# Where GpSimd's long subtractions stand in a unit, when ScalarE prepares x, and who mixes the streams of the last eight output tiles

## The reference

```python
# layer 1: windows of 128 columns, 8 heads of 32, D = 512
xn = layernorm(x)                       # over the 2048 columns
q, k = Wq @ xn + bq, Wk @ xn + bk       # E = 256
v = Wv @ ctx + bv
attn = softmax(mask(q^T k / sqrt(32)))
x = x + tanh(g_xattn) * (Wo @ gelu(attn v) + bo) * mask
# layer 2: each row of 2048 is 4 streams of 512
z = layernorm(x)
logits = rmsnorm(z) @ [W_res, W_pre, W_post]^T + base
H_res = sinkhorn_log(logits_res, num_iters=50, tau=0.1)   # 4x4 per row
H_res = (1 - g) * I + g * H_res
x_pre = einsum('btnc,btn->btc', z_streams, softmax(logits_pre))
y = x_pre @ W_branch
x = x + tanh(g_ffn) * (einsum(H_res, z_streams) + y * softmax(logits_post))
```

## Time and profile before

| | |
|---|---|
| median of 3 runs | 1816.63 us |
| profiled execution, its own time | 1819.56 us |
| its span | 1817.4 us |
| VectorE busy | 1337.7 us (74%) |
| TensorE busy | 1348.6 us (74%) |
| ScalarE busy | 1130.6 us (62%) |
| GpSimd busy | 818.0 us (45%) |
| TensorE's mean granted clock | 0.904 |

### The profile page before, as it was taken

How to read it: one execution, slowest core, us unless ns; L and a number is a source line. 1 busy time by engine, 2 the same in 40 slices (tenths; PEclk the granted TensorE clock), 3 DMA queues, 4 the chain that set the end, 5 groups by cost and what they waited for, 6 DMA issues and landing times.

```text
span 1817.4 us, 35773 instructions
## 1 busy us (share of the span) xinstructions
PE 1348.6 (74%) x12292; PEld 839.2 (46%) x12448; DVE 1337.7 (74%) x3566; ACT 1130.6 (62%) x2273; POOL 818.0 (45%) x1373
## 2 busy tenths in 40 slices
PE   2679999988788888887988788888888876512223
PEld 0446566555455555554555455555555553301011
DVE  3334433666579877988798878987798878779987
ACT  3457777777677757776677757775777765311111
POOL 3224335354646563656455655657365634420000
PEclk9789999999999989999999989999999997755556
DMA  8457676666566766776677657775667553321122
GB/s 253 134 144 206 186 190 185 176 173 188 166 173 192 199 186 187 198 203 176 187 201 196 174 152 200 199 198 156 176 181 181 144 135 105 93 81 58 58 99 109
DMA packets 175460, 299.89 MB, mean 165 GB/s; under 512 B 25105, under 2 KB 76177, under 8 KB 171185
## 3 DMA queue, kind: packets, MB, share of 16 engines
q1 hardware_dynamic: 157872, 264.04, 48.1%
q0 software_dynamic: 17408, 33.56, 10.6%
HBM read 179.81 MB, written 67.11 MB: 136 GB/s over the span
## 4 chain that ended last, share of the span: by engine, by line
DVE 34%; PE 18%; ACT 16%; issue 15%; POOL 14%; SPq 2%; DMA 2%; POOLq 0%; ACTq 0%; DVEq 0%
PE pr L660 7%; POOL kp L561 6%; DVE ssum L1212 6%; DVE otile_even L1241 4%; ACT squares L923 3%; DVE xpre L1229 3%; DVE otile_odd L1241 3%; DVE sa L1213 3%; DVE negm L1090 2%; PE pr L674 2%; DVE sv L1213 2%; ACT xt L915 2%; POOL x1c L503 2%; DVE otile_even L1257 2%; ACT probs L883 2%
## 5 line engine op out<-in xcount | busy, mean ns | idle before, releaser
L1212 DVE TENSOR_REDUCE ssum<-kp 128x16 f32<-128x64 f32 x768 | 181.3, 236 | 123.6 <-POOL kp L561 119.2
L561 POOL TENSOR_TENSOR kp<-ke,sa 128x64 f32<-128x64 f32 x343 | 152.7, 445 | 247.5 <-DVE sa L1213 247.5
L561 POOL TENSOR_TENSOR kp<-ke,sv 128x64 f32<-128x64 f32 x329 | 149.1, 453 | 199.8 <-DVE sv L1213 199.1
L774 PE MATMUL av_ps<-probs,v_t 128*32 128x128 f32 x2048 | 111.3, 287 | 153.8 <-DVE o_sb L1098 151.0
L660 PE MATMUL pr<-x_hl,wq 128*128 128x512 bf16 x707 | 180.7, 403 | 43.3 <-POOL x_hl L484 36.0
L883 ACT ACTIVATE probs<-st_ps,key_bias 128x512 f32<-128x512 f32 x256 | 173.0, 676 | 63.0 <-PE st_ps L761 62.9
L1098 DVE TENSOR_TENSOR o_sb<-av_ps,rden 128x128 f32<-128x128 f32 x256 | 72.9, 285 | 177.9 <-ACT rden L892 173.8
L1090 DVE TENSOR_REDUCE negm<-s_ps 128x4 bf16<-128x512 f32 x256 | 166.2, 649 | 49.8 <-PE s_ps L747 49.6
L484 POOL TENSOR_TENSOR x_hl<-xc,x_hl 128x512 bf16<-128x512 f32 x128 | 151.5, 1183 | 106.0 <-ACT x_hl L851 106.0
L674 PE MATMUL pr<-wv,ctx_hl 128*128 128x256 bf16 x1536 | 182.3, 276 | 21.0 <-DVE k_hl L1075 17.9
L687 PE MATMUL pr<-o_sb,wo 128*128 128x512 bf16 x705 | 181.7, 385 | 12.2 <-DVE x1c L1108 5.0
(11 more groups left out here) (149 smaller groups left out, 3066.7 us busy)
## 6 DMA issues: line engine op xcount, KB each, us to landing
xs<-in_dram SPq DMA_DIRECT2D x128, 256.0 KB, 5.7
xc<-in_dram SPq DMA_DIRECT2D x128, 256.0 KB, 4.0
ctx_raw<-in_dram SPq DMA_DIRECT2D x32, 1024.0 KB, 7.6
x1c<-in_dram POOLq DMA_DIRECT2D x64, 512.0 KB, 7.5
x_dram<-x1c SPq DMA_DIRECT2D x32, 1024.0 KB, 4.2
q_st<-q_hl SPq DMA_DIRECT2D x384, 64.0 KB
k_st<-k_hl SPq DMA_DIRECT2D x384, 64.0 KB
x1t_even<-x_dram SPq DMA_DIRECT2D x16, 1024.0 KB, 6.5
```

The costliest lines, as they stand in the source:

```text
L561: nc.gpsimd.tensor_tensor(kp[:], ke[:], v, ALU.mult).then_inc(kp_made, 1)
L774: nc.tensor.matmul(av_ps[rows, 0:W], v_t[:, G % 2, w, et * P + h * DH:et * P + (h + 1) * DH], probs[:, k % 2, h * W:(h + 1) * W], start=Tr ...
L1212: cf.link(nc.vector.tensor_reduce(s_t, k, AX.X, ALU.add))
```

## The change

1. `split_x`, `split_ctx` and `low_gelu`: the first long subtraction of a unit (ctx at r1 to r3, gelu at r4, x at r6 and r7) moves from slot 2 or 3 into slot 1. `add_x` of r7 moves from slot 2 to slot 3. At r5 no long one is left; r1 gets one in slot 3.
2. `HI_X_AT`, `LOW_X_AT`, `SQUARES_AT`: ScalarE's `norm_x` with `hi_x` moves from r1, r4, r5, r6 to r0, r1, r5, r6, and one of the two squares of r3 to r4. `LOAD_X_AT` is computed from `LOW_X_AT`, so SyncE's loads of `xc` move too (to r2, r4, r7 and the next r0).
3. The statistics: `stat_b`'s nine-operation part is cut in five (slot 2) and four (slot 3) at u13, its second part in four and four at u14, its third part moves from u15 to slot 3 of u16; `variance` moves to the end of u14 and `xstat` from u16 to u15.
4. The last eight tiles: ScalarE makes five diagonal matrices of 128x128 a tile (`diagonals`; they lie in `ctx_raw`), and TensorE multiplies blocks of `x1t` by them and adds the bias with `ones`, 20 float32 products a tile (`mix_pre`), half of them at the end of the step before. `first_products`, `make_xpre` and the transposes of these tiles are gone.

```diff
-HI_X_AT, LOW_X_AT = [1, 4, 5, 6], [3, 5, 6, 7]
+HI_X_AT, LOW_X_AT = [0, 1, 5, 6], [1, 3, 6, 7]
...
-SQUARES_AT = [3, 3, 4, 4]
+SQUARES_AT = [3, 4, 4, 4]
...
-BEHIND = dict(load=-5, first=-3, xpre=-3, pre=-2, branch_0=-1, branch_1=-1, out_0=-1, out_1=0,
+BEHIND = dict(load=-5, diag=-3, mix=-2, branch_0=-1, branch_1=-1, out_0=-1, out_1=0,
...
+    made += [("mix", f, t) for f, t in tiles_at(g, "mix")]
+    assert len(made) < 2
...
+        diag = ctx_raw[:, 0:2 * (N + 1) * P // CH + 1, :].rearrange("p t c -> p (t c)")[:, 0:2 * (N + 1) * P]
+        diag = diag.rearrange("p (k n c) -> p k n c", k=2, n=N + 1)
...
-            def stat_b(f, part):
+            def moments(f, part):
...
+                else:
                    cp.link(nc.gpsimd.tensor_tensor(r[:, 0, :], sums1[:, 0], sums1[:, 0], ALU.mult))
...
+            def scale_b(f, part):
+                r = rb[:, f % 3]
...
+            def norm_b(f):
+                r = rb[:, f % 3]
+                pool.wait_ge(rs_req, 2 * f + 2)
+                pool.wait_ge(rs_done, 4 * f + 4)
+                newton(r[:, 5, :], r[:, 2, :], r[:, 4, :], r[:, 1, :])
+                nc.gpsimd.tensor_tensor(r[:, 5, :], r[:, 5, :], r[:, 3, :], ALU.mult).then_inc(rb_ready, 1)
...
                 for ready in ffn_at(g, COEF_AT):
                     coefficients(ready)
-                scale_at(f, its, 1)
 
                 low = at_step(g, -1, LOW_CTX_AT)
                 for H, t in low[:1]:
                     split_ctx(H, t)
                 if 0 <= G - 1 < NG and r == 4:
                     low_gelu(G - 1, 0)
-                if 0 <= G - 1 < NG and r == 7:
-                    add_x(G - 1, 0)
+                if r in (6, 7):
+                    for H, t in at_step(g, -2, LOW_X_AT):
+                        split_x(H, t)
+                scale_at(f, its, 1)
                 if 0 <= G - 2 < NG and r == 0:
                     add_x(G - 2, 1)
                 if g >= 0 and u == 15 and b + 1 < B:
-                    variance(b + 1)
-                if g >= 0 and u == 16 and b + 1 < B:
                     xstat(b + 1)
-                for part in range(3):
-                    for ready in ffn_at(g, STAT_AT + 1 + part):
-                        stat_b(ready, part)
+                for ready in ffn_at(g, STAT_AT + 1):
+                    moments(ready, 0)
+                for ready in ffn_at(g, STAT_AT + 2):
+                    scale_b(ready, 0)
                 scale_at(f, its, 2)
                 for H, t in low[1:]:
                     split_ctx(H, t)
                 if 0 <= G - 1 < NG and r == 4:
                     low_gelu(G - 1, 1)
-                for H, t in at_step(g, -2, LOW_X_AT):
-                    split_x(H, t)
+                if 0 <= G - 1 < NG and r == 7:
+                    add_x(G - 1, 0)
+                if r not in (6, 7):
+                    for H, t in at_step(g, -2, LOW_X_AT):
+                        split_x(H, t)
+                for ready in ffn_at(g, STAT_AT + 1):
+                    moments(ready, 1)
+                for ready in ffn_at(g, STAT_AT + 2):
+                    scale_b(ready, 1)
+                for ready in ffn_at(g, STAT_AT + 4):
+                    norm_b(ready)
                 scale_at(f, its, 3)
+                if g >= 0 and u == 14 and b + 1 < B:
+                    variance(b + 1)
...
+            def mix_pre(what, part):
+
+                kind, f, t = what
+                n = DT * f + t
+                if part == 0:
+                    pe.wait_ge(x1t_loaded[n % 2], 16 * (n // 2 + 1))
+                    pe.wait_ge(diag_made, n - DT * (LAST_BESIDE + 1) + 1)
+                for j in (2 * part, 2 * part + 1):
+                    block = bank(what)[:, j * P:(j + 1) * P]
+                    for i in range(N):
+                        at = i * C + j * P
+                        nc.tensor.matmul(block, x1t[n % 2][:, at:at + P], diag[:, n % 2, i, :], start=(i == 0),
+                                         stop=False)
+                    ins = nc.tensor.matmul(block, ones[:], diag[:, n % 2, N, :], start=False, stop=True)
+                if part:
+                    ins.then_inc(bank_full, 1)
...
-                for f in ffn_at(g, UPC + SELECT_AT - 1):
-                    bank_free(("sel", f, 0))
-                    select(("sel", f, 0), 0)
+                for what in banked_at(g + 1):
+                    if what[0] == "sel":
+                        bank_free(what)
+                        select(what, 0)
+                    elif what[0] == "mix":
+                        bank_free(what)
+                        mix_pre(what, 0)
...
+            def diagonals(f, t):
+                n = DT * f + t
+                if t == 0:
+                    act.wait_ge(pre_ready, f + 1)
+                if n >= DT * (LAST_BESIDE + 1) + 2:
+                    f0, t0 = divmod(n - 2, DT)
+                    act.wait_ge(bank_full, PLACE["mix", f0, t0] + 1)
+                for i in range(N):
+                    nc.scalar.activation(diag[:, n % 2, i, :], id_sb[:], ACT.Identity, scale=pre[:, f % 3, t, i:i + 1])
+                nc.scalar.activation(diag[:, n % 2, N, :], id_sb[:], ACT.Identity, scale=rb[:, f % 3, 6, t:t + 1]
+                                     ).then_inc(diag_made, 1)
...
+                if pair == 0:
+                    act.wait_ge(x1t_loaded[n % 2], 16 * (n // 2 + 1))
...
+                for done, t in tiles_at(g, "diag"):
+                    diagonals(done, t)
...
-                if g >= 0 and u == 15 and b + 1 < B:
+                if g >= 0 and u == 14 and b + 1 < B:
                     xstat(b + 1)
```

19 lines of the change are left out of this document (9 added, 10 removed).

## The result

The changed kernel takes 1790.74 us (median of 4 runs, 1786.82 to 1796.25), the kernel before 1817.16: a ratio of 0.9853 [0.9818, 0.9887], 26.7 us faster. The forecast was 1759 in a range of 1736 to 1797, so the time lies inside the range, with less than half of the gain that was forecast.

What follows compares the result with a forecast made beforehand. TensorE and ScalarE were taken to bound early chunks; VectorE, chained with GpSimd, the middle; VectorE most of the tail. Terms -11 - 21 - 8 - 18 = -58 us took the profiled 1819.6 to 1761.6, median 1759, range 1736 to 1797.

Steps and rivals of the forecast that it cites:

- Tail: Last eight tiles: `xpre` products leave VectorE for a mix on TensorE, and the last tiles' chain shortens: -18 us.
- my lower bound of 4.7: Last three tiles: the mix's 40 passes take 4.7 to 10.9 us a tile; 7.5 was used.
- The rival at half clock: Last three tiles: TensorE's mix runs at half clock, +4 us in place of -8, 1771 in all; chance 0.13.
- Long operations: Middle chunks: moving GpSimd's long operations beside PSUM reads frees VectorE's streams, -0.7 us a chunk, -11 us in all.
- +0.45 of r1: Unit r1 of a middle chunk: `xpre` streams newly held in slot 3, slot 2 freed, slot 1 paid: +0.45 us.
- -0.6 of r5: Unit r5 of a middle chunk: no long operation is left there, so VectorE saves 0.6 us.
- Statistics: Units u13 to u16: VectorE's waits behind GpSimd's chains fall by 4.2 us a batch, -21 us; bounds -12 and -33.
- my list: Expected waits of VectorE's sums in u13 to u16 after the change: about 1.1, 0, 1.0 and 0 us.
- ScalarE: Early chunks and softmax units: moving `norm_x` and `hi_x` off r4 saves 0.7 us a chunk, -8 us; bounds +5 and -17.
- Only the tail and the stalls move: Whole kernel: long operations and ScalarE's respread give nothing, statistics their lower bound, -12 - 15 = 1790 us; chance 0.2.
- The slower rival: Slot 1: late ScalarE puts the long operation into the chain with its full length, 1828 us; chance 0.06.

Runs made afterwards that it cites:

- 10: The kernel before with the new tail and the long subtractions and `add_x` in their new slots, statistics and ScalarE's tables as before: 1784.2 us, ratio 0.9799.
- kernel 1: The kernel before with the new tail alone, for the last eight tiles: 1802.7 us, ratio 0.9926.
- kernel 2: The changed kernel with ScalarE's tables, GpSimd's long subtraction of x and SyncE's loads put back as before: 1763.3 us, ratio 0.9707.
- kernel 5: The changed kernel with only the squares put back to r3, r3, r4, r4: 1769.3 us, ratio 0.9726.
- 9: The kernel before with the new tail and the regrouped statistics, long subtractions and ScalarE's tables as before: 1790.7 us, ratio 0.9837.
- kernel 8: The changed kernel with 7 unused matmuls in TensorE's idle time before the k product, in every chunk from the second on: 1785.7 us, ratio 0.9811.
- kernel 7: The changed kernel with only the long subtraction of x at r1 moved to r2: 1791.1 us, ratio 0.9845.
- 13: The changed kernel with 6 unused matmuls in TensorE's idle time before the v product of r4, from the third batch on: 1789.5 us, ratio 0.9849.
- 14: The changed kernel with unused matmuls before both the k and the v product, from the third batch on: 1788.7 us, ratio 0.9846.
- kernel 6: The changed kernel with `norm_x`, `hi_x` and the long subtractions of x put back, squares as changed: 1767.0 us, ratio 0.9711.

## Why the prediction came out too good

**Tail, right, in part by luck.** -18 forecast, -18.3 measured. Its terms were off and made up for each other. The last tile's mix, copy, `branch` and additions in the changed kernel:

```profile
1765.98 1.13 PE L773 MATMUL pr<-ctx_raw,x1t_odd 128*128 128x128 f32 x8 [1.33 <-DMA x1t_odd<-x_dram]
...
1770.72 0.60 ACT L1031 ACTIVATE xpt<-pr 128x512 f32<-128x512 f32 x1 [5.54 <-PE pr L775]
...
1771.37 3.70 PE L831 MATMUL f<-wb,xpt 128*128 128x512 f32 x8 [0.69 <-ACT xpt L1031]
...
1775.97 2.73 DVE L1321 SCALAR_TENSOR_TENSOR otile_odd<-f,post,otile_odd 128x512 f32<-128x512 f32 x4
```

VectorE's waits for `branch` in the changed kernel, 1600 to 1790 us:

```profile
DVE otile_odd L1321 <- PE f L831: 0.2, 1, 0.2
DVE otile_even L1321 <- PE f L831: 0.2, 1, 0.2
```

The mix takes 4.7 us (1765.98 to the copy at 1770.72), 0.118 us a pass, my lower bound of 4.7; I took 7.5. `branch` took 3.70 against 6.22 us, and VectorE waits 0.2 us for it, not 3.2. The mix on TensorE took 24 products from VectorE, and `branch` behind it ran at full clock; over the last 87.5 us the granted clock is 0.73, before 0.60. But from the last `maximum` to the end VectorE's busy time fell by 16.5 us (243.6 to 227.1), which is nearly all of the gain. Its waits for `branch` fell from 7.6 to 0.4 us, and its waits for ScalarE rose by about as much, from 4.3 to 11.3: the forecast had no such term. The rival at half clock did not come.

**Long operations, right in kind, too small.** -11 forecast, -23.1 measured (10 against 1, give or take 7). By unit in chunk 4 of kernel 2: r1 to r4 -0.07 to -0.08 (forecast -0.05), r6 -0.56 (-0.6), r7 -0.39, where I had 0 for `add_x` in slot 3. The long x stands at r3 and r5 there and not at r1, so neither the +0.45 of r1 nor the -0.6 of r5 is due. Where it stands as in the change (5), r1 takes 0.38 us more than before and r5 0.28 less, and chunk 4 takes 46.0 for 47.1: 1.1 us, where I took 0.7. In kernel 2 it is 1.25 us a chunk, which in 3.25 chunks of five batches makes 20. The term that was too small is `add_x` at r7.

**Statistics, right in kind, between forecast and lower bound.** -21 forecast with -12 as the bound, -16.2 measured (9 against 1, give or take 7). The waits of VectorE's sums in u13 to u16 of kernel 2:

```profile
828.39 0.22 DVE L1276 TENSOR_REDUCE ssum<-kp 128x16 f32<-128x64 f32 x1 [1.36 <-POOL kp L575]
831.28 0.26 DVE L1276 TENSOR_REDUCE ssum<-kp 128x16 f32<-128x64 f32 x1 [0.46 <-POOL kp L575]
835.37 0.22 DVE L1276 TENSOR_REDUCE ssum<-kp 128x16 f32<-128x64 f32 x1 [0.19 <-POOL kp L575]
842.24 0.22 DVE L1276 TENSOR_REDUCE ssum<-kp 128x16 f32<-128x64 f32 x1 [1.27 <-POOL kp L575]
```

And those of the changed kernel, ahead of them the first operation of the statistics on GpSimd:

```profile
841.18 0.48 POOL L541 TENSOR_TENSOR sums<-sums 128x8 f32<-128x8 f32 x2 [2.22 <-ACT squares L971]
842.97 0.22 DVE L1276 TENSOR_REDUCE ssum<-kp 128x16 f32<-128x64 f32 x1 [2.83 <-POOL kp L575]
848.85 0.22 DVE L1276 TENSOR_REDUCE ssum<-kp 128x16 f32<-128x64 f32 x1 [0.19 <-POOL kp L575]
855.72 0.22 DVE L1276 TENSOR_REDUCE ssum<-kp 128x16 f32<-128x64 f32 x1 [1.27 <-POOL kp L575]
```

6.6 us of waits a batch became 3.3, where I had 2.1. Five times 3.3 are the 16. In the changed kernel the first one is 2.83 and not 1.1: GpSimd waits 2.22 us for the last square, which ScalarE makes behind the late v product. This wait was not in my list; the move of a square to r4 and the statistics at u13, an r5, meet there.

**ScalarE, wrong, and the step that failed.** "-0.7 a chunk ... **-8 us**; bounds +5 (all given back at r0 and r1) and -17." It cost 26.5 us here (give or take 7), and 12 to 40 beside other parts: not even the sign was right. I read that ScalarE had no gap at the head of r4 in the early stretch and priced the move by that. There it holds: an early chunk fell from 37.4 to 36.9 us. For the middle the term has no such reading; the earlier trace rows gave only the busy sum (34.8 of 47.1 us), and I never asked what `norm_x` and the square stood in front of. At r4 they filled ScalarE's wait for the v product, where they cost nothing. The square now stands behind that product, ahead of the exponentials that `divide` of r5 waits for: from `v_t` to the exponentials it is 5.1 us (741.54 to 746.66), 4.3 in kernel 2. The `norm_x` took its long subtraction on GpSimd along, from r3 and r5 to r1 and r3. And the two moves together slowed products of TensorE, for which the forecast had no term. The four full batches lose 24.0 us (773.6 against 749.6), by the units' durations:
- 14.9 between the changed kernel and kernel 8, where the slow products of chunks 2 and 4 are mostly gone: the clock;
- 9.1 between kernel 8 and kernel 2. Of these 6.1 stand at r1, where the long x holds the `xpre` (6.52 us a unit, 6.06 in kernel 7 without it), and 3.6 at r2 of chunk 3 (9.40 us for 8.45), where VectorE's four 128x32 operations on `logit` take 3.97 us beside the long ones of GpSimd, 3.02 in kernel 2. The other units make nothing together: r5 is longer, by ScalarE's queue, and r4 of chunks 1 and 3 shorter.

So the queue that I first took for the cost is small in sum. That both moves together, beside the new slots, bring the slow products is shown; why the clock falls at just these products stays open, and 13 and 14 show that its part can't be taken out singly. Outside these batches the start costs about 3 us more. ScalarE's wait for `xc` in the first 76 us of the changed kernel (total, times, longest):

```profile
ACT xc L892 <- DMA xc<-in_dram: 8.3, 1, 8.3
```

In the kernel before (2.3 us in kernel 6, with `norm_x` back):

```profile
ACT xc L844 <- DMA xc<-in_dram: 2.9, 1, 2.9
```

`norm_x` at r0 needs its load earlier than the start of the program delivers it. The nine kernels with `norm_x` at r0 wait 8.0 to 8.6 us for `xc` and reach their first `maximum` at 79.6 to 83.2 us, the others wait 2.0 to 3.1 and reach it at 75.4 to 77.3, but for kernel 1 (79.7).

**The rivals.** "Only the tail and the stalls move" gave 1790 and the kernel took 1790.7, but that is luck: it counted nothing for the long operations, which gave 23 us, and no loss for ScalarE's move, which cost 26. The slower rival named the right suspect, a late ScalarE, at the wrong place: the stall was at `divide`, not in slot 1. Without ScalarE's part my sum was -50; kernel 2 gave -53.2 [-56.5, -50.0], with one term larger and one smaller than forecast. That kernel, at 1763.3, beats the kernel before and the changed one and is the version to keep.

## What to carry to other kernels

Work of an engine that isn't the bound has a place as well as a length. Before moving it, find the wait that it stands in front of: work in an idle gap is free, and the same work behind the awaited transfer or product delays what the engine does next, unless there is room again. Ask also what moves along with it: here the long subtraction and a load did. A table of busy time per unit of the kernel before (6.13 of 6.19, 5.14 of 6.20, 5.52 of 5.58) shows what a sum over the chunk (34.8 of 47.1) hides: r5, which got the square to wait for, was full already. Where a change has several parts, build the one without each part: three parts that gained 53 us hid one that cost 27.

## What the runs showed of the hardware

- Behind idle times of 1.90 and 1.85 us the granted clock was 0.62 over TensorE's next product in the changed kernel (12 matmuls took 4.45 us for 2.76, 24 took 4.46 for 2.79). In kernel 5 the same products behind the same idle times had 1.00.
- With seven matmuls (1.67 us) added in such a gap the k product behind it ran at full clock, and four batches took 758.7 us for 773.6. The program gained 7.6 us by the medians, which its interval doesn't part from nothing. With a second filler in front of the v product, both from the third batch on, the four batches took 766.1.
- A float32 product of 128x128 with a weight load each took 0.235 us at full clock (4.7 us for 20), twice the 0.118 of a pass in the earlier trace rows.
- A slow product costs nothing where nobody waits: kernel 2 has a k product of 4.45 us in an r3 of 6.11 us, as long as the r3 of kernel 8 without it (6.12).
